# Decoder layer on one core: expert halves made in the first iteration, and the cross-attention value product with values as stationary operand

## What is computed

```python
x = x + self_attention(layernorm(x))            # causal, rotary
x = x + cross_attention(layernorm(x), ctx)      # 100 queries, 722 keys
gates = softmax(layernorm(x) @ gate_w.T + gate_b)
top, idx = top_k(gates, 2)
out = x + sum_of_two(top * (layernorm(x) @ expert_w[idx].T + expert_b[idx]))
```

## Time and profile before

| | |
|---|---|
| median of three runs | 1280.93 us (1279.38 to 1281.05) |
| profiled execution, its own time | 1280.48 us |
| its span, first to last instruction | 1278.7 us |
| PE busy / PEld busy | 1194.4 us (93%) / 806.8 us (63%) |
| DVE / ACT / POOL busy | 830.7 / 642.2 / 729.6 us |
| mean granted TensorE clock | 0.975 |

### The profile page before, as it was taken

The page is one execution under the profiler, slowest core; times in us unless marked ns, Lnnn a source line. Parts: engine busy times, 40 slices in busy tenths (PEclk is TensorE's granted clock), DMA queues, the critical chain, the costliest instruction groups (busy, mean ns, idle before and its releaser), DMA issues.

```text
span 1278.7 us, 43327 instructions
## 1 busy us (share of the span) xinstructions
PE 1194.4 (93%) x19120; PEld 806.8 (63%) x19120; DVE 830.7 (65%) x1455; ACT 642.2 (50%) x946; POOL 729.6 (57%) x690
## 2 busy tenths in 40 slices
PE   4789899999999999999999999999999877699997
PEld 4456576767667676767676767676767555555543
DVE  4658476858585867676767777677777586423156
ACT  4335556556565656565656464646565535533300
POOL 1436656667676766667675857575757455500042
PEclk9799999999999999999999999999999988799999
DMA  8010611010202010101011110101010345455356
GB/s 302 2 42 2 240 44 50 3 59 3 66 4 65 17 44 9 53 17 52 19 50 32 38 48 12 43 17 52 17 58 11 116 159 190 146 159 170 131 163 212
DMA packets 47840, 93.28 MB, mean 73 GB/s; under 512 B 3775, under 2 KB 15351, under 8 KB 47655
## 3 DMA queue, kind: packets, MB, share of 16 engines
q1 hardware_dynamic: 44135, 79.03, 18.7%
q0 software_dynamic: 3520, 11.47, 2.9%
HBM read 60.13 MB, written 30.36 MB: 71 GB/s over the span
## 4 chain that ended last, share of the span: by engine, by line
PE 86%; DVE 4%; DMA 3%; POOL 3%; ACT 2%; issue 1%; another core or an unknown queue 1%; SPq 1%; ACTq 0%; DVEq 0%
PE psum L323 56%; PE psum L922 7%; PE psum L1025 6%; PE psum L1010 5%; PE psum L940 2%; PE psum L899 2%; PE psum L891 1%; DMA bank<-in_L_attn_Wv 1%; DMA out<-bank 1%; PE psum L967 1%; PE psum L855 1%; PE psum L907 1%; DVE xT L1176 1%; POOL bank L1444 1%
## 5 line engine op out<-in xcount | busy, mean ns | idle before, releaser
L1444 POOL TENSOR_TENSOR bank<-prob,bank 128x1200 f16<-128x1200 f32 x128 | 314.6, 2468 | 188.4 <-ACT bank L1120 188.3
L1268 DVE TENSOR_REDUCE c_most<-psum 100x4 f32<-100x1444 f32 x128 | 211.6, 1653 | 14.7 <-PE psum L1010 12.6
L323 PE MATMUL psum<-bank,cT 128*128 128x512 f16 (+1 forms) x864 | 198.7, 379 | 0.1
L323 PE MATMUL psum<-cT,bank 128*128 128x361 f16 x1152 | 196.1, 321 | 0.0
L1111 ACT ACTIVATE prob<-psum 128x1200 f32<-128x1200 f32 x128 | 150.0, 1172 | 76.6 <-PE psum L1025 62.4
L1176 DVE TENSOR_TENSOR cv<-psum,cv 128x512 f16<-128x512 f32 x125 | 86.0, 688 | 107.4 <-ACT cv L1102 57.2
L1120 ACT ACTIVATE bank<-prob 128x1200 f16<-128x1200 f32 x128 | 151.7, 1198 | 1.4
L323 PEld LDWEIGHTS psum<-cT,bank 128*128 128x128 f16 x1152 | 106.1, 99 | 65.5 <-DVE c_raw L1195 3.0
L323 PEld LDWEIGHTS psum<-bank,cT 128*128 128x128 f16 (+1 forms) x864 | 85.1, 101 | 88.2 <-issue 4.1
L1102 ACT ACTIVATE cv<-psum 128x512 f16<-128x512 f32 x96 | 57.4, 598 | 149.9 <-PE psum L323 148.3
L1229 DVE SCALAR_TENSOR_TENSOR bank<-psum,b_part,bank 128x361 f16<-128x361 f32 x128 | 74.4, 592 | 81.1 <-ACT bank L1088 81.1
(11 more groups left out here) (215 smaller groups left out, 1905.8 us busy)
## 6 DMA issues: line engine op xcount, KB each, us to landing
c_raw<-in_ctx SPq DMA_DIRECT2D x16, 960.0 KB
xs_scratch<-y_kept SPq DMA_DIRECT2D x1, 7424.0 KB, 22.8
c_raw<-xs_scratch SPq DMA_DIRECT2D x29, 256.0 KB, 2.7
ys_scratch<-bank SPq DMA_DIRECT2D x29, 256.0 KB, 2.0
bank<-in_L_ffn_expert_w SPq DMA_DIRECT2D x7, 1024.0 KB, 7.7
x_in<-in_x SPq DMA_DIRECT2D x16, 200.0 KB
x_scratch<-x_out SPq DMA_DIRECT2D x16, 200.0 KB
y_kept<-x_scratch SPq DMA_DIRECT2D x10, 256.0 KB, 3.2
```

Source lines behind the costliest of these rows:

```text
L323: last = pe.matmul(out_ap, a(pa), b(pb), start=(i == 0 and j == 0), stop=(i == len(pairs) - 1 and j == 2))
L1268: dve.tensor_reduce(c_most[:, hf], score[0:L, :, 0:HC], AXIS.X, ALU.max).then_inc(max_done, 1)
L1444: pool.tensor_tensor(prob16[o % 2][:, (2 + part) * PT:(3 + part) * PT], prob[:, part], prob16[o % 2][:, part * PT:(part + 1) * PT], ALU.su ...
```

## The change

Four things are changed.

- The FW chunks move from iteration 15 to iteration -1 (FIRST_EXTRA: expert e in steps 2e+2 and 2e+3). SP loads raw experts into two buffers (load_raw), each freed by the expert two before; halves are made in two others (w_made, in the probabilities' space) and stored to memory (store_made). In iterations 14 and 15 load_expert brings the halves back, straight to their places.
- PV has the values as stationary operand, 32 columns a head on four column groups, and 100 query columns of probabilities moving: 72 matmuls for the three products of halves, and 48 with ones, whose result is the row sum spread over the head's 32 rows. The result comes out turned, [head x 32, query].
- DVE takes the reciprocal of 128 x 100 sums and multiplies; TH on ACT and TL on POOL split the result into tT, per group. scale_heads and TT are gone.
- Order: TP goes from step 11 to step 6 (in iteration 14 from 7 to 5), TH0/TL0 stand at the end of step 10, the gate's extras of iteration 14 one or two steps earlier, SC1 in iteration 14 instead of 15. The memset of the keys' padding moves to the last step of iteration -1.

```diff
@@ STEPS
-    ["MX0", "CX2", "CX3", "rotate_k", "CX4"],
+    ["MX0", "CX2", "CX3", "rotate_k", "CX4", "TH2", "TL2"],
     ["T0a", "exp0a", "CX5", "PV3"],
-    ["T0b", "SS0", "SS1", "exp0b", "shift0", "scale_heads", "max_A1", "CK0"],
+    ["T0b", "SS0", "SS1", "exp0b", "shift0", "max_A1", "CK0", "TH3", "TL3"],
     ["A1", "CK1", "shift1", "CK2"],
-    ["B1", "high0a", "max_B1", "TT", "low0a", "self_exp0", "SV"],
+    ["B1", "high0a", "max_B1", "low0a", "self_exp0", "SV", "TP"],
...
-    ["A2", "max_A2", "self_scale1", "self_exp1", "self_sum1", "SP0", "CV1"],
-    ["B2", "SP1", "self_scale2", "high1a", "self_scale3", "max_B2", "TP", "high1b", "low1a", "SP2", "SP3",
+    ["A2", "max_A2", "self_scale1", "self_exp1", "self_sum1", "SP0", "CV1", "TH0", "TL0"],
+    ["B2", "SP1", "self_scale2", "high1a", "self_scale3", "max_B2", "high1b", "low1a", "SP2", "SP3",
      "CV2", "low1b"],
...
-    ["T3a", "exp3a", "stats_x", "CQ", "norm_x", "high3a"],
+    ["T3a", "exp3a", "stats_x", "CQ", "norm_x", "high3a", "TH1", "TL1"],
...
-GATE_EXTRA = {10: ["FS10"], 11: ["FN10"], 12: ["FX10"], 13: ["FL10"], 14: ["RT00", "RE0"], 15: ["RT01"], 16: ["RT02"],
-              17: ["RT03", "RP"], 18: ["FR"], 19: ["SC0"]}
+GATE_EXTRA = {9: ["FS10", "FN10"], 11: ["FX10"], 12: ["FL10"], 13: ["RT00", "RE0"], 14: ["RT01"], 15: ["RT02"],
+              16: ["RT03", "RP"], 17: ["FR"], 18: ["SC0"], 19: ["SC1"]}
+FIRST_EXTRA = {2: ["FG0"], 7: ["BV0", "BV1"]}
+for e in range(E):
+    for k in range(KD):
+        FIRST_EXTRA.setdefault(2 * e + 2 + k // 2, []).append(f"FW{e}{k}")
...
@@ SP
+        def load_raw(sp, e):
+            if e >= 2:
+                sp.wait_ge(chunk_out, its[-1].done(f"FW{e - 2}{KD - 1}"))
+            sp.dma_start(raw_e[e % 2], eW[e].rearrange("(o p) h -> p o h", p=P)).then_inc(raw_e_loaded[e % 2], 16)
+
+        def store_made(sp, e):
+            sp.wait_ge(chunk_out, its[-1].done(f"FW{e}{KD - 1}"))
+            sp.dma_start(wT_dram[e], prob16[e % 2][:, 0:KD * 2 * D]).then_inc(w_stored[e % 2], 16)
...
+            if n < 0:
+                for e in range(6):
+                    store_made(sp, e)
+                    load_raw(sp, e + 2)
             if n < B - 2:
                 sp.wait_ge(chunk_out, it.done("SO"))
                 load_ctx(sp, n + 2)
                 sp.wait_ge(chunk_out, it.done("OP"))
                 load_x(sp, n + 2)
+            if n < 0:
+                for e in range(6, E):
+                    store_made(sp, e)
...
@@ PE, kind == "PV"
-                for c in range(HT):
                     for t in range(CT):
-                        r = CLAST if t == CT - 1 else CW
-                        for p in range(2):
-                            at = ((p * 2 + t // 3) * HT + c) * 3 * L + t % 3 * L
-                            last = pe.matmul(f[:, c * HV:(c + 1) * HV], prob16[i % 2][0:r, at:at + P],
-                                             cv[odd][0:r, t, HT * i + c, 0:HV],
-                                             start=t + p == 0, stop=t + p == CT)
...
+                        for c in range(HT):
+                            p, r = tile(pp, t, c)
+                            last = pe.matmul(f[DH * c:DH * (c + 1), 0:L], cv_half[odd][0:r, t, HT * i + c, pv], p,
+                                             start=a + t == 0, stop=a == 2 and t == CT - 1)
+                for pp in range(2):
+                    for t in range(CT):
+                        for c in range(HT):
+                            p, r = tile(pp, t, c)
+                            last = pe.matmul(f[DH * c:DH * (c + 1), L:2 * L], ones16[0:r, 0:DH], p,
+                                             start=pp + t == 0, stop=pp == 1 and t == CT - 1)
...
@@ ACT, FW and TH
+                if e == 1:
+                    act.wait_ge(w_low, 2)
+                elif e >= 2:
+                    act.wait_ge(w_stored[e % 2], 16 * (e // 2))
...
+            act.wait_ge(chunk_out, (its[n + 1] if g == GROUPS - 1 else its[n]).done(f"PV{g}"))
+            act.activation(tT[:, 0, g], head_out[g % 2][:], ACT.Copy).then_inc(head_high, 1)
...
@@ DVE, kind == "PV"
-                dve.tensor_reduce(c_out[:, HT * DH * i:HT * DH * (i + 1)].rearrange("q (c d) -> q c d", c=HT),
-                                  heads[:, :, 0:2 * DH].rearrange("q c (p d) -> q c d p", p=2), AXIS.X, ALU.add)
-                op = dve.reciprocal(c_rinv[:, HT * i:HT * (i + 1)].unsqueeze(2), heads[:, :, 2 * DH:HV])
+                g = GROUPS * (n - 1 if i == GROUPS - 1 else n) + i
+                dve.reciprocal(head_rinv[:], f[:, L:2 * L]).then_inc(head_inv, 1)
+                dve.wait_ge(head_inv, g + 1)
+                if g >= 2:
+                    dve.wait_ge(head_split, g - 1)
+                op = dve.tensor_tensor(head_out[i % 2][:], f[:, 0:L], head_rinv[:], ALU.mult)
...
@@ POOL
+            pool.wait_ge(head_high, count)
+            pool.tensor_tensor(tT[:, 1, g], head_out[g % 2][:], tT[:, 0, g], ALU.subtract).then_inc(head_split, 1)
...
```

More of the change, by code:

```diff
@@ L80 @@
     ["MX3", "X2T", "low2b", "PV1"],
-    ["T3a", "exp3a", "stats_x", "CQ", "norm_x", "high3a"],
+    ["T3a", "exp3a", "stats_x", "CQ", "norm_x", "high3a", "TH1", "TL1"],
     ["T3b", "exp3b", "CK7", "split_cq", "PV2", "high3b"],
 ]
-TAIL = ("low3a", "low3b", "PV3", "scale_heads", "TT", "TP")
-CROSS = tuple(f"{w}{g}" for w in ("A", "B", "max_A", "max_B", "MX") for g in range(GROUPS)) + ("PV0", "PV1", "PV2") + tuple(
+TAIL = ("low3a", "low3b", "PV3", "TH2", "TL2", "TH3", "TL3", "TP")
+CROSS = tuple(f"{w}{g}" for w in ("A", "B", "max_A", "max_B", "MX") for g in range(GROUPS)) + ("PV0", "PV1", "PV2", "TH0", "TL0", "TH1", "TL1") + tuple(
     f"{w}{g}{p}" for w in ("T", "exp", "high", "low") for g in range(GROUPS) for p in "ab" if w != "low" or g < GROUPS - 1)
-CHUNKS = ("X1T", "X2T", "SQ", "SK", "CQ", "SV", "SO", "OP", "TT", "TP")
+CHUNKS = ("X1T", "X2T", "SQ", "SK", "CQ", "SV", "SO", "OP", "TP")
 CHUNK_KINDS = ("CX", "CK", "CV", "SS", "SP", "MX", "PV", "BV", "FX", "FG", "FW", "FL", "FR", "ST")
@@ new lines @@
+GATE_EXTRA = {9: ["FS10", "FN10"], 11: ["FX10"], 12: ["FL10"], 13: ["RT00", "RE0"], 14: ["RT01"], 15: ["RT02"],
[4 more added lines that the diff above has]
+        FIRST_EXTRA.setdefault(2 * e + 2 + k // 2, []).append(f"FW{e}{k}")
+LAST_STEPS = [
+    ["low3a", "A0", "max_A0"],
+    ["B0", "max_B0", "low3b"],
+    ["MX0", "SC2", "TH2", "TL2"],
+    ["T0a", "exp0a", "PV3", "SC3", "PL"],
+    ["T0b", "exp0b", "high0a", "TH3", "TL3"],
+    ["A1", "max_A1", "low0a", "high0b"],
+    ["B1", "max_B1", "low0b", "TP"],
+    ["MX1", "SC4"],
+    ["T1a", "exp1a", "SC5"],
+    ["T1b", "exp1b", "high1a", "PV0"],
+    ["A2", "max_A2", "low1a", "high1b", "TH0", "TL0"],
+    ["B2", "max_B2", "low1b"],
+    ["MX2", "SC6", "FS11"],
+    ["T2a", "exp2a", "FN11", "SC7"],
+    ["T2b", "exp2b", "high2a", "PV1"],
+    ["A3", "max_A3", "low2a", "high2b", "FX11", "TH1", "TL1"],
+    ["B3", "max_B3", "low2b", "FL11"],
+    ["MX3", "SC8"],
+    ["T3a", "exp3a", "SC9"],
+    ["T3b", "exp3b", "high3a", "PV2", "high3b", "SC10"],
@@ L153, in steps_of @@
         return END_STEPS
-    every = [list(step) for step in (moved(STEPS, "TP", 7) if n == B - 2 else STEPS)]
+    every = [list(step) for step in (moved(STEPS, "TP", 5) if n == B - 2 else STEPS)]
     for t in range(EARLY - 1):
@@ L162, in steps_of @@
     return every
-SPLIT = ("X1T", "SV", "SP0", "SP1", "SP2", "SP3", "SO", "X2T", "TT") + tuple(
+SPLIT = ("X1T", "SV", "SP0", "SP1", "SP2", "SP3", "SO", "X2T") + tuple(
     [f"MX{g}" for g in range(GROUPS)] + [f"CX{c}" for c in range(6)] + ["FG0"] + [f"FW{e}{k}" for e in range(E) for k in range(KD)] + [f"FX{t}" for t in range(TILES)] + [f"CK{c}" for c in range(8)] + [f"CV{c}" for c in range(6)] +
@@ L385, in build_layer @@
         e_loaded = [sem(f"e_loaded{e}") for e in range(E)]
+        raw_e_loaded = [sem(f"raw_e_loaded{i}") for i in range(2)]
+        w_stored = [sem(f"w_stored{i}") for i in range(2)]
         f_bn, f_stats, f_half, f_rstd, f_norm = (sem(n) for n in ("f_bn", "f_stats", "f_half", "f_rstd", "f_norm"))
@@ L532, in pe_slots @@
                 pe.wait_ge(experts_ready, 1)
+                for e in range(E):
+                    pe.wait_ge(e_loaded[e], 16)
             pe.wait_ge(chunk_out, its[B].done(f"ST{j}"))
@@ L758, in sync_iteration @@
                 sp.wait_ge(chunk_out, it.done("SV"))
-                for e in range(2):
+                for e in range(3):
                     load_expert(sp, e)
@@ L786, in last_loads @@
             sp.wait_ge(exp_done, 2 * GROUPS * (B - 1))
-            for e in range(3, E - 1):
+            for e in range(4, E):
                 load_expert(sp, e)
             for t in range(4, EARLY):
-                if t == 8:
+                if t == 9:
                     sp.wait_ge(chunk_out, it.done("TP"))
@@ L799, in end_loads @@
             all_scattered(sp)
-            sp.wait_ge(chunk_out, its[B - 1].done("FW73"))
+            sp.wait_ge(chunk_out, its[B - 2].done("SO"))
```

(4 more changed lines are left out.)

106 lines of the change are left out of this document (47 added, 59 removed).

## The result

The changed kernel takes 1387.8 us (median of 4 runs, 1386.96 to 1394.46) against 1281.0 (4 runs): 1.0848 times the time before, 95% interval 1.0813 to 1.0883. I had forecast 1297 and a range that ended at 1314. The profiled execution takes 1387.34 us, 106.8 more than the 1280.5 of before. I cut both traces at A0 of each iteration; the last stretch but one ends at the first slot tile.

The account below looks back on a forecast made before the run. PE's instruction stream was taken to bound iterations 1 to 13, with looser first and last iterations. 22.1 + 1.2 + 11 - 2 - 16 - 0.5 = +15.8 on 1280.5 gave 1296.3, forecast 1297 us; range 1269 to 1314.

Parts of the forecast that it names:

- Value product on PE: Each product's 120 matmuls run at SO's 11.5 ns, 1.5 us in all; -0.1 us an iteration.
- TP and TL0: Steady iterations: SP2 and SP3 wait uncovered for POOL's self_scale2, delayed by TL0; 2.0 us an iteration, bounds 1.0 and 2.4.
- Rival A: SP2's wait is covered by something and not paid; 1269 us in all, chance 0.20.
- TT, product and eviction: Steady iteration: TT gone -0.4 us, product -0.1, longer DVE eviction making SQ wait for X1T +0.2.
- First iteration: n = -1: 32 expert chunks on PE +9 us, waiting for expert transfers +2; together +11, ends +7 and +20.
- Rival B: First iteration bound by its DMA traffic: +25 us in place of +11, 1311 in all, chance 0.12.
- Iteration 14: Extra 1.0 us at SP2, 0.4 gained from TT, FX10's 2.81 us wait gone: -2 us, bounds -4 to +1.
- Last iteration: n = 15, A0 to first slot tile: POOL's queue sets 56 us against 72.2; -16, bounds -10 and -21.

Follow-up runs that it names:

- long_burst: Changed kernel with PV0's 72 value matmuls issued sixteen times over in iterations 6, 8 and 10; the first run's 1200 matmuls took 32.8 us.
- few_wide: Changed kernel with 48 matmuls of 250 columns in each product in place of 120 of 100, low-half products left out; 1333.01 us, ratio 1.0393.
- tp_late: Changed kernel with TP back in step 11, in front of SP2, and TH0 and TL0 moved to step 12; 1357.8 us, ratio 1.0587.
- tp_early_before: Kernel before with one edit, TP in step 7 instead of step 11 in every iteration; 1296.48 us, ratio 1.0121.
- first_quiet: Changed kernel with two raw expert loads and two stores in the first iteration instead of eight and eight; A0 of n = 0 at 106.9 us.
- no_scatter: Changed kernel without GpSimd's indirect DMAs for tiles 2 to 10; 56.8 us from A0 of n = 15 to first slot tile, against 69.2; 1378.1 us.
- spread: tp_late with each product cut into two chunks, row sums and values, placed between long matmuls; 1385.65 us, ratio 1.0819.
- paired: Kernel before with only the new value product, in tp_late's order, each product in 72 matmuls instead of 120; 1319.32 us, ratio 1.0313.
- pool_busy: no_scatter with three plain GpSimd copies in place of each tile's two scatters; 53.6 us from A0 of n = 15 to first slot tile; 1375.8 us.
- paired_early: paired with PV2 issued before CK7 instead of behind it; 1313.6 us, ratio 1.0261.
- paired_psum: paired_early with the two halves of the values' product added into PSUM, one more VectorE instruction; 1309.12 us, ratio 1.0198.

## Why the prediction was wrong, by its own steps

**Value product on PE: the step that failed.** I took SO's 11.5 ns as the price of 120 matmuls and put the supply of instructions at nothing. The pace is right within a block (11.4 ns in long_burst; product 1.5 us without its stop), but it is a pace that instruction supply does not sustain: 27.1 ns. SO's 48 matmuls are less than half a block, so the earlier trace rows could not show the limit; product and score bursts together fill one or two blocks. Sized by few_wide, some 45 us of the 106.8 are such stops. The Trainium skill's 25 ns (TensorE: Matmul & The Clock Gate, "Wait — 56ns, not 53.3ns?"), which I set against the trace, gave an estimate of about 1390: its time nearly came out, but not by its mechanism, as matmuls start 11.4 ns apart and the loss comes in stops, of 0.2 to 1.8 us in the steady stretch. Another page of the Trainium skill bears on it (Runtime: NRT & Kernel Launch, "Instruction fetch mechanics"): instructions are refilled in blocks of 16 KiB, 256 of them, while the one before runs, and crossing a boundary is mostly hidden. The block size agrees with the runs here (stops 125 to 128 matmuls apart, 16.4 KB a packet), and a packet does move while a block runs; the hiding does not agree, as a block used up in 1.65 us was followed by the next after 3.47.

**TP and TL0: right.** Forecast 2.0 us an iteration with bounds 1.0 and 2.4; tp_late gives 2.3, of which tp_early_before gives 1.2 to the cover. But I had it as idle time alone: that is 1.4 us, and part of the rest is the clock falling behind it, which my sum did not have. With the stops out (few_wide), n = 1 to 13 cost 25.8 us against my 22.1, some 30 if its shorter streaming is put back. Rival A falls.

**TT, product and eviction: the savings were eaten up.** In the seven iterations at full clock PE's own work is 0.6 to 0.9 us longer than before, where I had -0.5. An estimate for the difference: PE stands about five times more often in an iteration, and each time a tail of some 0.2 us is left that nothing overlaps, 1.0 us in all; no run tries that alone. The reciprocal over 100 columns is shorter than my 0.91 us, and the multiply than my 0.31:

```profile
L1313 DVE RECIPROCAL head_rinv<-psum 128x100 f32<-128x100 f32 x64 | 49.8, 779 | 81.5 <-PE psum L962 79.5 <-remote 1.9
L1317 DVE TENSOR_TENSOR head_out<-psum,head_rinv 128x100 f32<-128x100 f32 x64 | 16.8, 262 | 2.2
```

**First iteration: right mechanism, size off.** +17.5 against +11, inside the bounds. PE's work grew by 16.9 us, 0.53 a chunk instead of 0.45. Idle time took up 4.6 us of it where most transfers were left out (first_quiet), near my 5.3 (3.5 and four early chunks), and none in after. So the chunks cost 12.0 us and not 9, and the transfers 5 to 9 and not 2. Rival B, the traffic as bound, is a third to a half of it.

**Iteration 14: wrong sign.** PE's wait of 2.81 us for FX10 went, as forecast, but PE's idle time in this iteration went from 7.4 to 14.5 us. The two costliest new waits begin here:

```profile
1105.35 0.41 PE L962 MATMUL psum<-bank,ones 128*32 128x100 f16 x20 [3.77 <-issue]
...
1110.60 0.69 DVE L1346 BATCH_NORM_STATS2 stats<-y_kept 128x6 f32<-128x512 f32 x1 [3.70 <-DMA y_kept<-x_scratch]
```

The stop of 3.77 us falls into the three expert loads, while the DMA engines are 0.93 busy (1101.0 to 1105.4 us); the instruction packet starts only at 1103.12. VectorE waits for FS10's rows: SP issues their load at 1107.80, after 8.8 us of waiting for the store of those rows, which stands behind the three expert loads; the maximum of A2 is behind it, and PE waits 2.7 us for that. few_wide, with 2.9 us of issue waits in this iteration against 5.9, still loses 6.9 us. That is read from the traces, not tried alone.

**Last iteration: the second failed step.** I let the chain over four engines run beside GpSimd's queue, took the chain for the shorter of the two, and put what scatters do to the chain at nothing. no_scatter measures the chain by itself, 56.8 us, with GpSimd busy for 24.5. That it meets my 56 is chance: mine was GpSimd's queue with 22.4 us of scatters in it. The hold of some 12 us comes on top. The trace of before shows such a hold:

```profile
1111.33 1.17 ACT L1111 ACTIVATE prob<-psum 128x1200 f32<-128x1200 f32 x1 [7.04 <-remote]
```

Its scores were there at 1106.4, and it began 1.6 us after the last scatter of the earlier trace rows had ended. I had put GpSimd's waits for the high halves behind it down to ScalarE's work on the expert chunks.

## What to carry to other kernels

Where a change multiplies small instructions, price it twice: at the pace of one and at the rate at which blocks of instructions follow each other, counted over the whole burst that it joins, its neighbours too. Moving such work out of the burst did not help here, as it was the cover for waits there (spread); fewer, longer instructions took the stops away both times they were tried (few_wide, paired). An uncovered wait can cost more than its idle time, where the clock falls behind it. When a wait is put down to an unknown releaser, look for what ends each time just before it.

## What the hardware showed that I had not expected

- TensorE ran 128 matmuls and their weight loads in 1.65 us and then stood 1.82 us for the next block of instructions, with no DMA traffic but one instruction packet a block (long_burst).
- The granted clock fell to half within 0.9 us of the end of two waits of 1.14 and 0.29 us at SP2 and SP3, in five of thirteen iterations of after and six of few_wide; behind waits of at most 0.4 and 0.3 us there (tp_early_before) it never fell.
- Exponentials of ScalarE started only 0.4 to 1.6 us after runs of GpSimd scatters ended, up to 5.6 us after their scores were there (after); plain GpSimd copies in the scatters' place held nothing (pool_busy).
- A VectorE multiply with both operands in SBUF took 2.55 us beside a GpSimd subtraction (paired_early), 0.26 with one in PSUM (after, paired_psum). The Trainium skill (SBUF — State Buffer, "SBUF: two separate sides") states such a lock between the two engines, for an operation with two SBUF inputs; the trace agrees.
